# Attention and expert kernel: transpositions of softmax rows in halves, values pair by pair, one copy moved in ScalarE's list

## The chip, the cores and the metric

The kernel runs on one core of a Trainium2 chip. Its time is the device time of one execution in microseconds; given is the median of three runs. TensorE multiplies matrices and writes to PSUM, VectorE, ScalarE and GpSimd (POOL in the profile) work on SBUF and PSUM, and SyncE issues transfers. Each engine runs its own list in order; semaphores join the lists.

## What is computed

```python
xn = _layernorm(x, axis=-1)                      # x: 8 batches x 256 rows x 128
q, k, v = ...                                    # 16 heads of 64; k, v from a latent of 64
q = q * cos + _rotate_half(q) * sin              # the same for k
scores = q @ k.T / 8, causal mask
probs = softmax(scores)
s = (probs @ v).reshape(...) @ wo.T
g = silu(TOP_K * expert_of_each_row(xn))         # one of 8 experts, 128 -> 512 -> 128
out = x + s * g
```

All of it is float32. The change touches the step from `probs` to `probs @ v`.

## The kernel before

Work goes by **pairs** of heads: 8 batches x 8 pairs = 64 pairs, numbered g = 0 to 63. Every engine has a hand-written list, made of one `slot(g)` per pair; what stands in a slot of one engine belongs to different pairs, so that the engines overlap. For one pair, with both heads i = 0, 1 and 256 rows in two blocks of 128 (the causal half leaves 128 + 256 = 384 columns, `SW`):

- `scores` (TensorE, L1187 and L1189): head i lies on partitions 64 i to 64 i + 63, so each multiplication uses 64 rows of the array, and the two heads stand side by side on its two halves. Results go to banks `s_bank[i]`.
- `row_max` (VectorE, L633) masks and takes the negated maximum of rows; `exponentials` (ScalarE, L975) makes `pexp` and the row sums, two instructions a head, each with the read-out of its sum; `denominators` (VectorE, L640) is the reciprocal; `scale` (GpSimd L499, ScalarE L988, or VectorE L651) writes `probs`. In the stage of the change ScalarE scales one quarter of a pair (128x128), GpSimd three.
- `turn` (TensorE, L1199) transposes `probs` in three blocks 128x128 a head into `t_bank[i]`; `turned_probs` (ScalarE, L997) copies each head's bank to `probsT`, one of four buffers.
- `values` (TensorE, L1216 and L1218) multiplies by the latents, two pairs at once, the two heads on the two halves of the array's columns; `ctx_out` (ScalarE, L1004) copies the result, `output` (TensorE, L1233) multiplies by the joined value and output weights.
- `project` (TensorE, L1161 to L1178) makes rotary inputs of a pair eight later, VectorE (L617, L624) and GpSimd (L488) rotate, SyncE stores (L388).

Pairs 0 to 39 come first, then the experts, then pairs 40 to 63. **Periods** (`PERIODS` = 42, 44, ..., 56) join the slots of an even pair s and of s + 1 into one list on TensorE (`period`, L1335): scores s + 2; values of s - 2 and s - 1; scores s + 3; `turn(s)`; projection s + 8; outputs s - 2 and s - 1; `turn(s + 1)`; projection s + 9. In period 42 `turn(42)` stands before scores 45 and no values are computed. Projections end with 63.

ScalarE's slot g (L1085): exponentials of g + 1 for head 0; exponentials of g + 1 for head 1; in an even slot of a period the context copy of g - 2; `turned_probs(g)`; its quarter of `scale(g + 1)`. GpSimd's slot: its parts of `scale(g + 1)`, in even slots a rotation, and from slot 43 to 58 one gather of gate rows (L515). VectorE's slot in a period: `row_max(g + 2)`, rotation, `denominators(g + 1)`; in a few slots two instructions of a finished batch.

Of the kernel before, what the change touches and what calls it, by code (L numbers as in the profile page):

```python
# [16 lines left out]
P = 128  # L17
# [42 lines left out]

LATE = B * NP - 2
VECTOR_CTX = (LATE - 6, LATE - 4)


def values_through(g):
# [50 lines left out]
def build(nc, x, wqT, w_dgT, w_kupT, w_vup, woT, gate_b, w1, b1, w2, b2,  # L116
          c_rot, c_ident, c_mask, c_before, c_expert, c_excl, c_incl, c_tile, out):
    with ExitStack() as ctx:
# [207 lines left out]
        def take_turns(eng, g, i, k):  # L326

            if g and scaler(g - 1, i, k) != scaler(g, i, k):
                eng.wait_ge(probs_ready[i][k], g)

        def turned_to(u):

# [635 lines left out]
        def _(act):  # L968
# [22 lines left out]
            def turned_probs(g):  # L991

                if g > 3:
                    act.wait_ge(pv_done, values_through(g - 4))
                for i in range(2):
                    act.wait_ge(probsT_done, 2 * g + i + 1)
                    act.copy(probsT[:, g % 4, i, :], t_bank[i][:, 0:SW]).then_inc(probsT_ready, 1)  # L997
# [87 lines left out]
            def slot(g):  # L1085
                if g in (4, 8, 12):
                    turned(g // 4 + 1)
                if g in (5, 9, 13):
                    latents_high(g // 4 + 1)
                if g in (7, 11, 15):  # L1090
                    latents_copied(g // 4)
                if g == COUNT_SLOT + 1:
                    act.wait_ge(cnt_done, 1)
                    act.copy(counts[:], w_bank[:, 0:(NT + 1) * E]).then_inc(cnt_read, 1)
                more = g + 1 < B * NP and g != G_LEAD
                if g == G_LEAD:
                    act.wait_ge(e_done, NR)
                    turned_probs(g)
                    exponentials(g + 2, 0)
                    turned_probs(g + 1)  # L1100
                    exponentials(g + 2, 1)
                    half_tanh(NR - 1, 1)
                more = more and g != G_LEAD + 1
                if more:
                    exponentials(g + 1, 0)
                if g > 1 and g - 2 in ALONE and g not in (G_LEAD, G_LEAD + 1):
                    ctx_out(g - 2)
                if g % 2 and g > 2 and g - 3 not in ALONE and g < LATE - 3 and g != G_LEAD + 1 and not in_period(g):
                    ctx_out(g - 3)
                if more:  # L1110
                    exponentials(g + 1, 1)
                if g in PERIODS:
                    ctx_out(g - 2)
                if g == LATE:
                    ctx_out(g - 2)
                if g == LATE + 1:
                    act.wait_ge(probsT_ready, 2 * g)
                if g not in (G_LEAD, G_LEAD + 1, LATE):
                    turned_probs(g)
                if g + 1 < B * NP and g != G_LEAD:  # L1120
                    scale(g + 1)
                if g in (2, 6, 10):
                    normalise(g // 4 + 2)
                if g in (5, 9, 13):
                    logits_out(g // 4 + 1)
# [31 lines left out]
        def _(pe):  # L1157
# [33 lines left out]

            def turn(g):

                for i in range(2):
                    wait(pe, probsT_ready, 2 * g + i - 1)
                    for k in range(3):
                        if k < 2:
                            pe.wait_ge(probs_ready[i][k], g + 1)
                        t = pe.transpose(t_bank[i][:, k * P:(k + 1) * P], probs[:, g % 2, i, k * P:(k + 1) * P], ident[:])  # L1199
                    t.then_inc(probsT_done, 1)  # L1200

            def values(g):
# [6 lines left out]
                    pe.wait_ge(rope_done, B * NP)  # L1209
                else:  # L1210
                    wait(pe, ctx_ready, values_through(min(g, LATE)) - 1)
                pe.wait_ge(probsT_ready, 2 * (g + n))
                pairs = slice(g % 4, g % 4 + n)
                o = (w_bank if g == LATE else o_bank)[:, 0:n * S].rearrange("p (n s) -> p n s", s=S)
                for i, r in enumerate(half_rows):
                    pe.matmul(o[r, :, :], lat_all[:, 2 * b, :], probsT[:, pairs, i, 0:S], start=True, stop=False)  # L1216
                for i, r in enumerate(half_rows):
                    m = pe.matmul(o[r, :, P:S], lat_all[:, 2 * b + 1, :], probsT[:, pairs, i, S:SW], start=False, stop=True)  # L1218
                m.then_inc(pv_done, 1)

            def output(g):
# [113 lines left out]
            def period(s):  # L1335
# [11 lines left out]
                    output(s - 3)  # L1347
                output(s - 2)
                output(s - 1)
                turn(s + 1)  # L1350
                for m in items(s + 1):
                    project(m)
                for m in items(s)[1:]:
                    project(m)

            def slot(g):
                if in_period(g):
# [21 lines left out]
                if g == G_LEAD:  # L1379
                    turn(g + 1)  # L1380
                elif g == G_LEAD + 1:
                    values(g - 1)
                else:
                    turn(g)
                if g in (3, 7, 11):
                    turn_rows(g // 4 + 2)
# [11 lines left out]
                    values(g - 1)  # L1398
                if g > 1 and g % 2 == 0 and g - 2 not in ALONE and g not in (G_LEAD, G_LEAD + 2):
                    values(g - 2)  # L1400
                for m in items(g)[1:]:
                    project(m)

# [85 lines left out]
```

## Time and profile before

| | |
|---|---|
| median of 3 runs | 302.62 us (302.54 to 303.06) |
| the profiled execution's own time | 303.29 us |
| its span in the trace | 301.5 us |
| TensorE busy / instructions | 289.6 us (96%) / 2362 |
| ScalarE busy | 239.3 us (79%) |
| VectorE busy | 229.7 us (76%) |
| GpSimd busy | 213.5 us (71%) |
| TensorE's granted clock | 1.00 in all stretches |

The page gives busy times over the whole span, the costliest groups of instructions, and what ended the idle time before them. A table by stage gives the same for chosen stretches. The view in order of time lists instructions with start and duration in us, neighbours of one kind merged ("x6"); a group's time runs from its first start to its last end. Multiplications overlap in these records, so a group of n has n - 1 steps and one record's length. The stage of the change lies from about 226 us to 278 us.

### The profile page before, as it was taken

To read this page: it belongs to the slowest core of one execution; us is meant where nothing else is said; L and a number is where in the kernel's file an instruction comes from. 1 tells how busy PE (TensorE), PEld (TensorE's weight loads), DVE (VectorE), ACT (ScalarE), POOL (GpSimd) and SP (SyncE) were. 2 spreads that over 40 slices of the span, in tenths; PEclk is the share of its full clock that TensorE was granted. 3 is DMA by queue.
4 is the path that set the end of the run, shared out by engine and by line. 5 is a ranking of instruction groups with operands and counts; after the bars stand their busy time and mean duration, and the time that the engine had idled before them with its cause. 6 is when DMAs were issued, how large, how long until landed. Compare 5 with 4: busy or idle time off the path is not lost.

```text
span 301.5 us, 8603 instructions
## 1 busy us (share of the span) xinstructions
PE 289.6 (96%) x2362; PEld 235.0 (78%) x2362; DVE 229.7 (76%) x909; ACT 239.3 (79%) x863; POOL 213.5 (71%) x325
## 2 busy tenths in 40 slices
PE   8798999999999999999999989999999999999994
PEld 2576888888888888777776779999977778887663
DVE  4889998987777898988898723444377889898981
ACT  4278789898887889989998676677787898999971
POOL 2478878697778669999999982333226899998730
PEclk9999999999999999999999999999999999999999
DMA  6864685879333233444333382000234243543410
GB/s 192 249 133 115 114 276 148 205 194 300 87 75 68 60 75 83 107 101 102 90 97 90 112 245 55 2 0 2 66 93 108 64 113 99 121 106 109 113 37 17
DMA packets 39596, 33.35 MB, mean 111 GB/s; under 512 B 4801, under 2 KB 36674, under 8 KB 39554
## 3 DMA queue, kind: packets, MB, share of 16 engines
q1 hardware_dynamic: 38098, 30.51, 39.8%
q0 software_dynamic: 1024, 2.10, 2.4%
q8 instruction: 20, 0.33, 0.5%
q10 hardware_dynamic: 432, 0.23, 0.3%
q14 instruction: 22, 0.18, 0.2%
HBM read 11.07 MB, written 4.98 MB: 53 GB/s over the span
## 4 chain that ended last, share of the span: by engine, by line
PE 64%; POOL 14%; DVE 9%; issue 6%; DMA 3%; ACT 1%; POOLq 0%; SPq 0%; DVEq 0%; ACTq 0%
PE bank L1199 9%; PE bank L1187 9%; PE bank L1216 8%; PE bank L1450 7%; PE bank L1438 6%; PE bank L1233 6%; POOL probs L499 5%; POOL staged L488 5%; PE bank L1161 3%; DVE rot_out L617 3%; PE bank L1218 3%; PE bank L1189 3%; POOL xn L515 3%; DMA qk_sb<-staged 3%; DVE masked L633 2%
## 5 line engine op out<-in xcount | busy, mean ns | idle before, releaser
L975 ACT ACTIVATE pexp<-masked,negmax 128x128 f32<-128x128 f32 (+1 forms) x256 | 113.9, 452 | 2.2 <-DVE negmax L633 2.2
L499 POOL TENSOR_SCALAR probs<-pexp,rden 128x128 f32<-128x128 f32 (+1 forms) x195 | 84.3, 447 | 27.0 <-DVE rden L640 25.2
L633 DVE CUSTOM_DVE_ANT_0 masked<-bank,mask 128x128 f32<-128x128 f32 (+1 forms) x256 | 75.9, 352 | 21.4 <-PE bank L1189 20.5
L488 POOL TENSOR_TENSOR staged<-rot_out 128x512 f32<-128x512 f32 x56 | 71.4, 1278 | 16.2 <-DVE rot_out L617 15.6
L617 DVE TENSOR_TENSOR rot_out<-bank,rot 128x1024 f32<-128x1024 f32 x64 | 77.7, 1215 | 4.6 <-PE bank L1163 3.5
L997 ACT COPY probsT<-bank 128x384 f32<-128x384 f32 x126 | 54.0, 480 | 27.3 <-PE bank L1199 26.0
L1199 PE MATMUL bank<-ident,probs 128*128 128x128 f32 x384 | 54.0, 275 | 0.7 <-issue 0.5
L975 ACT ACTIVATION_READ_ACCUMULATOR pexp<-masked,negmax 128x1 f32 x256 | 50.0, 195 | 0.0
L1187 PE MATMUL bank<-qk_sb 64*128 64x256 f32 x256 | 47.0, 428 | 1.7 <-DMA qk_sb<-staged 1.3
L1199 PEld LDWEIGHTS bank<-ident,probs 128*128 128x128 f32 x384 | 43.0, 140 | 3.4 <-issue 1.2
L1233 PE MATMUL bank<-vo_sb,ctxT 128*128 128x128 f32 x256 | 37.8, 278 | 0.7 <-ACT ctxT L1004 0.7
L1216 PE MATMUL bank<-probsT,lat_all 128*64 128x256 f32 (+1 forms) x184 | 37.7, 487 | 0.0
L1145 ACT ACTIVATE probsT<-bank,w_own 128x128 f32<-128x128 f32 x88 | 25.0, 369 | 12.9 <-PE bank L1438 12.9
L1233 PEld LDWEIGHTS bank<-vo_sb,ctxT 128*128 128x128 f32 x256 | 33.0, 191 | 1.8 <-ACT ctxT L1004 1.1
L1187 PEld LDWEIGHTS bank<-qk_sb 64*128 64x128 f32 x256 | 20.6, 184 | 16.4 <-issue 11.6
L575 POOL COPY w_own<-w_sb 128x516 f32 x22 | 14.9, 678 | 23.6 <-ACT probsT L1145 23.6
L1189 PEld LDWEIGHTS bank<-qk_sb 64*128 64x128 f32 x256 | 26.1, 187 | 2.8
L1189 PE MATMUL bank<-qk_sb 64*128 64x128 f32 x256 | 26.8, 272 | 0.0
L954 DVE TENSOR_TENSOR z<-bank,b_all 128x128 f32 (+1 forms) x22 | 6.4, 292 | 24.2 <-PE bank L1450 21.7
L1218 PEld LDWEIGHTS bank<-probsT,lat_all 128*64 128x64 f32 x184 | 13.6, 137 | 13.9 <-issue 9.9
L1450 PE MATMUL bank<-w_sb,probsT 128*128 x176 | 23.3, 276 | 0.3 <-ACT probsT L1145 0.3
L1438 PE MATMUL bank<-probsT,w_own 128*128 128x128 f32 x176 | 23.3, 276 | 0.0
(117 smaller groups left out, 483.6 us busy)
## 6 DMA issues: line engine op xcount, KB each, us to landing
qk_sb<-staged SPq DMA_DIRECT2D x128, 128.0 KB
w_sb<-in_w SPq DMA_DIRECT2D x2, 1024.0 KB, 5.8
w_sb<-in_w SPq DMA_DIRECT2D x4, 512.0 KB, 5.3
sorted_x<-z SPq DMA_DIRECT2D x1, 1408.0 KB, 8.0
sorted_g<-z SPq DMA_DIRECT2D x1, 1152.0 KB, 5.5
out<-res SPq DMA_DIRECT2D x8, 128.0 KB, 2.3
x_sb<-in_x SPq DMA_DIRECT2D x3, 256.0 KB, 3.8
rot<-in_c_rot SPq DMA_DIRECT2D x1, 512.0 KB, 5.7
```

What stands on the lines that cost most here:

```text
L488: pool.tensor_tensor(staged[:, n % 2, :, m % 2, :], rot_out[:, m % 2, :, 0:S], rot_out[:, m % 2, :, S:2 * S], op=ALU.add).then_inc(staged_ ...
L499: pool.tensor_scalar(probs[:, g % 2, i, c], pexp[:, g % 2, i, c], rden[:, g % 2, i, k:k + 1], 1.0, ALU.mult, ALU.mult).then_inc(probs_read ...
L617: dve.tensor_tensor(rot_out[:, m % 2], bank_of(m)[:].unsqueeze(1).broadcast_to([P, 2, 2 * S]), rot[:], op=ALU.mult).then_inc(rope_done, 1)
L633: t = dve.tensor_tensor_reduce(masked[:, g % 2, i, c], s_bank[i][:, c], mask[:, c], -1.0, -NEG * 1e8, ALU.add, ALU.min, negmax[:, g % 2, i ...
L975: e = act.activation(pexp[:, g % 2, i, c], masked[:, g % 2, i, c], ACT.Exp, bias=negmax[:, g % 2, i, k:k + 1], scale=-1.0, accum_out=rowsu ...
L997: act.copy(probsT[:, g % 4, i, :], t_bank[i][:, 0:SW]).then_inc(probsT_ready, 1)
L1187: pe.matmul(s_bank[i][:, P:SW], qk_sb[r, 0, p, P:S], qk_sb[r, 1, p, :], start=True, stop=True)
L1189: m = pe.matmul(s_bank[i][:, 0:P], qk_sb[r, 0, p, 0:P], qk_sb[r, 1, p, 0:P], start=True, stop=True)
L1199: t = pe.transpose(t_bank[i][:, k * P:(k + 1) * P], probs[:, g % 2, i, k * P:(k + 1) * P], ident[:])
L1216: pe.matmul(o[r, :, :], lat_all[:, 2 * b, :], probsT[:, pairs, i, 0:S], start=True, stop=False)
L1233: m = pe.matmul(y_bank[:, i * C:(i + 1) * C], ctxT[:, p, i * P:(i + 1) * P], vo_sb[:, p, :], start=(p == 0 and i == 0), stop=(p == NP - 1) ...
L1450: m = pe.matmul(bank[6 + i][:, 0:C], hidT[:, i, k, :], w2_sb[:, k, :, :].rearrange("p e c -> p (e c)")[:, bass.ds(e * C, C)], start=(k == ...
```

## The change

1. `HALVED` holds pairs 43 to 56. For these `turn` transposes 64 rows at a time, twelve instructions instead of six; rows 0 to 63 of both heads go to `t_bank[0]`, rows 64 to 127 to `t_bank[1]`. ScalarE's two copies each wait for all transpositions of the pair and write strips of 64 columns.
2. `TURN_LAST` holds 43, 45, ..., 55. In `period` their `turn` moves from before to behind the projections, so that it stands next to the scores of the next period.
3. `values` of a joined couple (42, 43), ..., (54, 55) is split: first the even pair, after its copies, then the odd pair, after its own.
4. In ScalarE's list `turned_probs` of an odd pair moves from its own slot to the next one, between the exponentials of head 0 and head 1.

```diff
+TURN_LAST = (*range(PERIODS[0] + 1, PERIODS[-1], 2),)
+HALVED = (*TURN_LAST, *PERIODS[1:])
...
+        def turned_half(g, i):
+
+            whole = probsT[:, g % 4].rearrange("p i (k q c) -> p (i k) q c", q=2, c=HD)
+            return whole[:, :, i, :]
...
+                if g in HALVED:
+                    act.wait_ge(probsT_done, 2 * g + 2)
+                    for i in range(2):
+                        act.copy(turned_half(g, i), t_bank[i][:, 0:SW].rearrange("p (n c) -> p n c", c=HD)
+                                 ).then_inc(probsT_ready, 1)
+                    return
...
+                if g - 1 in TURN_LAST:
+                    turned_probs(g - 1)
                 if more:
                     exponentials(g + 1, 1)
...
-                if g not in (G_LEAD, G_LEAD + 1, LATE):
+                if g not in (G_LEAD, G_LEAD + 1, LATE) and g not in TURN_LAST:
                     turned_probs(g)
...
+                if g in HALVED:
+                    wait(pe, probsT_ready, 2 * g)
+                    for i in range(2):
+                        for k in range(3):
+                            if k < 2:
+                                pe.wait_ge(probs_ready[i][k], g + 1)
+                            for o, r in zip(t_bank, half_rows):
+                                t = pe.transpose(o[:, (3 * i + k) * HD:(3 * i + k + 1) * HD],
+                                                 probs[r, g % 2, i, k * P:(k + 1) * P], ident[r, r])
+                        t.then_inc(probsT_done, 1)
+                    return
...
-                pe.wait_ge(probsT_ready, 2 * (g + n))
-                pairs = slice(g % 4, g % 4 + n)
...
+                parts = ((g, 1), (g + 1, 1)) if g in PERIODS and g + 1 in TURN_LAST else ((g, n),)
+                for j, k in parts:
+                    pe.wait_ge(probsT_ready, 2 * (j + k))
+                    pairs = slice(j % 4, j % 4 + k)
+                    at = slice((j - g) * S, (j - g + k) * S)
...
-                turn(s + 1)
+                if s + 1 not in TURN_LAST:
+                    turn(s + 1)
                 for m in items(s + 1):
                     project(m)
                 for m in items(s)[1:]:
                     project(m)
+                if s + 1 in TURN_LAST:
+                    turn(s + 1)
```

Two more conditions on `TURN_LAST` stand in the ordinary slot of TensorE.

## Rows read from the trace of the kernel before

**Rows 1.** The page, busy time by engine (share of the span) and instructions.
```profile
PE 289.6 (96%) x2362; PEld 235.0 (78%) x2362; DVE 229.7 (76%) x909; ACT 239.3 (79%) x863; POOL 213.5 (71%) x325
```
**Rows 2.** Table by stretch, one period: length, busy by engine (PE, PEld, DVE, ACT, POOL), clock.
```profile
245.35:252.07 6.72, 6.72 (x56) 5.35 (x55) 5.80 (x23) 6.17 (x25) 6.33 (x10) 1.00 0.40 99
```
**Rows 3.** TensorE in order of time, 243.2 to 249.2: start, length, instructions.
```profile
243.24 1.05 PE L1233 MATMUL bank<-vo_sb,ctxT 128*128 128x128 f32 x8
244.13 0.82 PE L1199 MATMUL bank<-ident,probs 128*128 128x128 f32 x6
...
245.88 0.39 PE L1189 MATMUL bank<-qk_sb 64*128 64x128 f32 x4
246.24 1.08 PE L1216 MATMUL bank<-probsT,lat_all 128*64 128x512 f32 x4
247.12 0.63 PE L1218 MATMUL bank<-probsT,lat_all 128*64 128x256 f32 x4
247.68 0.70 PE L1187 MATMUL bank<-qk_sb 64*128 64x256 f32 x4
248.21 0.39 PE L1189 MATMUL bank<-qk_sb 64*128 64x128 f32 x4
248.53 0.87 PE L1199 MATMUL bank<-ident,probs 128*128 128x128 f32 x6
249.16 0.36 PE L1161 MATMUL bank<-xnT_h,wq_h 128*128 128x256 f32 x1
```
**Rows 4.** ScalarE in order of time, 242.4 to 249.2.
```profile
242.45 0.86 ACT L997 COPY probsT<-bank 128x384 f32<-128x384 f32 x2 [0.56 <-PE bank L1199]
243.19 0.41 ACT L988 ACTIVATE probs<-pexp,rden 128x128 f32<-128x128 f32 x1
243.50 0.40 ACT L975 ACTIVATE pexp<-masked,negmax 128x128 f32<-128x128 f32 x1
...
245.16 0.19 ACT L975 ACTIVATION_READ_ACCUMULATOR pexp<-masked,negmax 128x1 f32 x1
245.25 0.83 ACT L997 COPY probsT<-bank 128x384 f32<-128x384 f32 x2
...
249.17 0.86 ACT L997 COPY probsT<-bank 128x384 f32<-128x384 f32 x2 [0.55 <-PE bank L1199]
```
**Rows 5.** All transpositions L1199: ns minimum/median/maximum, first and last start.
```profile
L1199 PE MATMUL bank<-ident,probs x384: 270/273/331, 23.6 to 294.3; 128*128 128x128 f32 x192
```
**Rows 6.** Weight loads of the 8-row transpositions L1268: one group of four; one load's ns.
```profile
18.41 0.32 PEld L1268 LDWEIGHTS bank<-ident,z 8*128 8x128 f32 x4
...
L1268 PEld LDWEIGHTS bank<-ident,z x16: 133/136/138, 18.4 to 80.7; 8*128 8x128 f32 x16
```
**Rows 7.** TensorE in order of time: a projection that follows scores directly.
```profile
221.41 0.38 PE L1161 MATMUL bank<-xnT_h,wq_h 128*128 128x256 f32 x1
221.63 0.28 PE L1162 MATMUL bank<-xnT_l,wq_h 128*128 128x256 f32 x1
221.75 0.28 PE L1163 MATMUL bank<-xnT_h,wq_l 128*128 128x256 f32 x1
```
**Rows 8.** Reciprocals on VectorE and a scaling of ScalarE that waited for one.
```profile
245.39 0.18 DVE L640 RECIPROCAL rden<-rowsum 128x4 f32<-128x4 f32 x1
...
232.09 0.17 DVE L640 RECIPROCAL rden<-rowsum 128x4 f32<-128x4 f32 x1
...
232.35 0.40 ACT L988 ACTIVATE probs<-pexp,rden 128x128 f32<-128x128 f32 x1 [0.19 <-issue]
```
**Rows 9.** Copies of pairs 44 and 56; transpositions of 58 and GpSimd's scaling before them.
```profile
235.72 0.86 ACT L997 COPY probsT<-bank 128x384 f32<-128x384 f32 x2 [0.76 <-PE bank L1199]
...
276.11 0.86 ACT L997 COPY probsT<-bank 128x384 f32<-128x384 f32 x2 [0.56 <-PE bank L1199]
...
279.40 1.61 PE L1199 MATMUL bank<-ident,probs 128*128 128x128 f32 x6
...
279.68 0.83 POOL L499 TENSOR_SCALAR probs<-pexp,rden 128x128 f32<-128x128 f32 x2
```

## What the change should do to the time

> **What bounds the kernel now.** I read the busy shares first, then a table by stage, then one period of TensorE and one of ScalarE line by line. By the page TensorE is busy for 289.6 of 301.5 us [rows 1], so any instruction taken from it looks like time won. The stage that the change touches is the eight "periods" (pairs 42 to 57, about 226 to 278 us). One of them takes 6.72 us: TensorE busy 6.72, GpSimd 6.33, ScalarE 6.17, VectorE 5.80 [rows 2]. So TensorE is full, but nothing behind it has more than 0.6 us to spare, and the question is what is late next.
>
> The list of TensorE [rows 3] and that of ScalarE [rows 4] answer it. I name the pairs of one period: scores 50 ending with the group at 245.88, values 46 and 47 at 246.24, scores 51 at 247.68, transpositions of 48 at 248.53, projection at 249.16. Outputs (243.24) and the transpositions of 47 (244.13) stand before. ScalarE copies the transposed pair 46 at 242.45, scales a quarter of 47, takes the four exponentials of 48, and copies 47 at 245.25. The second of these copies ends at 245.25 + 0.83 = 246.08, and the values start 0.15 us later. So a loop runs through both engines:
>
> copies of 46 begin 242.45; ScalarE without a gap to 246.08 (3.63); hand-over 0.15; values 46/47 1.44 (246.24 to 247.68); scores 51 0.85 (to 248.53); transpositions of 48 until ScalarE copies them 0.64 (to 249.17). Sum 6.71, which is the period. TensorE itself waits only about 0.04 us in it: from the last score to the values it takes 0.24 us (245.88 + 0.39 - 0.27 = 246.00 to 246.24), from the last score to the transpositions, where nothing is awaited, 0.20 (248.33 to 248.53). TensorE's own list (about 6.68) and this loop (6.72) are level. An edit that shortens TensorE's list wins only if it leaves the loop alone.
>
> **The change, part by part.**
>
> *Transpositions by row halves.* For the 14 pairs 43 to 56, six transpositions 128x128 become twelve of 64 rows, two at a time on the two halves of the array. Now one takes a step of 0.109 us: (0.82 - 0.27) / 5, where 0.27 is the recorded time of one multiplication (the group at 244.13) [rows 3, 5]. The operand that streams, the identity, halves from 128 to 64 columns: 0.055. The weights loaded stay 128 columns wide. The nearest row is the group of transpositions with 8 rows and 8 columns: its weight loads alone make a step of (0.32 - 0.14) / 3 = 0.06 us [rows 6]. I take 0.061 for a step of two halves, because scores, which are already such pairs, show two halves as one step (four 128-column multiplications of 64 rows in 0.39, that is one further step of 0.11 after the first) (at 248.21) [rows 3]. Six steps: 0.37 for 0.65, so -0.29 per pair. Bounds: 0.055 a step if the load hides; 0.12 a step if the halves go one after the other, which is +0.07 instead of -0.29.
>
> The Trainium skill, "TensorE: Matmul & The Clock Gate", Part 3, says that a weight load overlaps a running matmul only when its row group differs. By that rule load and stream of one half would add up, about 0.11 a step, and nothing would be won in a transposition: 0.3 us more in the loop below. In this trace a full-array transposition loads new weights in the same rows every time, which alone takes 0.06 [rows 6], and still goes at the 0.11 that 128 columns cost in the scores [rows 3]; so the load is hidden, and the trace speaks against the rule here.
>
> *Their places.* Changing between full array and halves costs an emptying plus an uncovered weight load. Last score to first transposition is 0.20 us (248.21 + 0.39 - 0.27 = 248.33 to 248.53) for a step of 0.11, so 0.09, and the first transposition then takes 0.05 more (0.87 for six against 0.82) [rows 3]. After the change the transpositions of an even pair follow scores without a switch, and the switch comes before the projection, whose first step is 0.22 (221.41 to 221.63) for 0.12 in the next one (to 221.75) [rows 7]: 0.10, where the transposition had paid 0.05, so 0.05 dearer. For an odd pair the switch moves from before the scores to before the transpositions, and what the loads cost there is a wash. The number of switches, four a period, is the same. TensorE's list: 6.68 - 2 x 0.29 + 0.05 = 6.15 us, and 0.01 for the split below: 6.16.
>
> *Values pair by pair.* Four multiplications of 512 and four of 256 columns become eight of 256 and eight of 128; the columns are the same. In one piece they take 1.44 (0.88 from 246.24 to 247.12 and 0.56 to 247.68). The second pair alone is half of the streamed part plus the switch to the scores: steps of 0.24 and 0.22 for 256 columns, 0.11 for 128, and 0.24 from the last one to the scores, 0.80 in all (half of 1.44, and 0.08 for the switch that does not halve). The first pair needs only copies made long ago, the second those of the odd pair.
>
> *ScalarE's copies.* Copies of an odd pair leave the end of its own slot and go between the two heads of the next slot's exponentials. The list becomes: copies 46, quarter scale 47, exponentials 48, quarter scale 48, first head's exponentials of 49, copies 47, second head's, context copy, copies 48. Two things now stand ahead of copies 47 that stood behind. First, quarter scale 48 follows the exponentials of 48 directly, while its reciprocal on VectorE needs the last row sum. That ends at 245.16 + 0.19 = 245.35, 0.10 after ScalarE's next instruction could start (245.25) [rows 4]; the reciprocal can follow 0.03 later, as now at 245.39, and takes 0.18 [rows 8]; from its end to ScalarE's scaling is 0.08 where ScalarE stood waiting for just this (232.09 + 0.17 to 232.35) [rows 8]. So 0.39 us of ScalarE standing still, which copies 47 used to fill; bounds 0.3 and 0.5 (VectorE must have its rotation and sum before the reciprocal done by then; today they end just as the row sum does, and the projection that they wait for comes no later). Second, the scaling 0.31 (243.19 to 243.50) and half of 1.75 for the exponentials, 0.88 (243.50 to 245.25) [rows 4].
>
> Both copies of a halved pair wait for all of its transpositions, since each bank now holds half the rows of both heads. The start is no later, though: 5 x 0.061 + 0.22 (the 0.27 less the 0.055 of half the columns) + 0.10 for the hand-over (today the third transposition ends 248.53 + 0.05 + 0.22 + 0.27 = 249.07, the copy starts 249.17) = 0.63 after the first transposition, for 0.64 now. The copies write six strips of 64 instead of 384 in a row; no row shows that form, I take it at the price of a plain copy, with 0.1 us a pair as the upper bound and no gain below.
>
> *The new loop*, all from [rows 3, 4, 8]. Copies 46 0.74; scale 0.31; exponentials 48 1.75; standing still 0.39; scale 0.31; exponentials 49, first head 0.88; copies 47 0.83: 5.21 on ScalarE. Hand-over 0.15. Then on TensorE second pair of the values 0.80; scores 51 0.75 (0.85 less the switch after it, 0.10); transpositions of 48 to the copy 0.63. Sum **7.54 us** for 6.72 now. Taken out: the first pair of the values (0.64) and a switch. Put in: 0.39 + 0.31 + 0.88 = 1.58. TensorE, with 6.16 of work, would stand about 1.4 us a period before the values of the odd pair, and behind that wait are queued the scores, the next transpositions and projections, so nothing of it is made up.
>
> *How often, and the ends.* From the copies of 44 (235.72) to those of 56 (276.11) [rows 9] are six periods, 6.73 each: 6 x 0.81 = +4.9. In the first one (42 to 44) the quarter scale of 44 starts at 232.35 as now [rows 8], then 0.31 + 0.88 + 0.83 + 0.15 + 0.80 + 0.75 + 0.63 puts the copies of 44 at 236.70 instead of 235.72: +1.0. After the last one, now, the six transpositions of pair 58 take 1.61 us instead of 0.87, waiting for GpSimd's scaling, which stands behind a gather and ends at 279.68 + 0.83 [rows 9]. In longer periods GpSimd is no longer behind, and that wait goes in part; but the exponentials of 58 stay tied to the copies of 56, so I give back 0.4 (0 to 0.7). The other edits (conditions in the ordinary slots) touch no pair: 43 to 55 all lie in periods.
>
> Sum: 4.9 + 1.0 - 0.4 = +5.5. The profiled execution took 303.29 us (span 301.5 and 1.8 around it), which is 0.7 above the median 302.62 of the runs. On the median: **308.1 us**.
>
> **The rivals.**
> *Faster: TensorE's list is all that counts.* Mechanism: the split of the values covers the later copies, and each period shrinks to TensorE's 6.16. Then 7 x -0.56 and the 0.4 of the end: 298.3 us. For it: TensorE shows no idle time in the stage [rows 2]. Against it: it decides on whether copies 47 are done before the first pair of the values ends. Those end about 4.0 us after copies 46 began, and the copies at 5.21; 1.2 us of ScalarE's list would have to be absent.
> *Between: ScalarE's own list is the limit*, 6.17 of work plus 0.39 of standing still, 6.56 a period, if the two engines could drift apart: 7 x -0.16 - 0.4, 301.1 us. Against it: copies 48 cannot start before transpositions 48, which stand behind the values in TensorE's order.
> *Slower still: the halves go one after the other.* The even pair's transpositions lie in the loop: 6 x (0.12 - 0.06) = +0.36 in each of seven periods, 310.6 us; with the strips dearer as well, 311.3.
> That the change does not do what it says I find nowhere: the pairs named are those that the period's list issues.
>
> **How the numbers follow.** Forecast (period 7.4 to 7.7): 0.80, its own range 306.8 to 309.3. Halves in turn or dear copies: 0.10, near 310.6. TensorE's list alone: 0.05. ScalarE's list, or something near no change: 0.05. The range for 8 in 10 is 306.2 to 310.8. A measurement of this kernel can tell some 0.2% (0.6 us) from no change: faster 0.08, same 0.03, slower 0.89.
>
> **What would show it.** In the changed profile: starts of the copies of an even pair 7.5 us apart; TensorE idle 1.2 to 1.5 us inside the values, between a multiplication of 128 columns and one of 256, released by ScalarE's copy; ScalarE still for 0.4 us before a quarter scale in odd slots and for some 0.7 before the copies of an even pair; transpositions in six steps of 0.06; no switch pause between scores and transpositions; TensorE's busy share well below 96% in this stage. It is wrong if the odd pair's copies end before the first values do, if the reciprocal comes early enough to leave no pause, or if a step of two halves is not near 0.06.

## The result and the profile after

| | before | changed |
|---|---|---|
| median of the runs, us | 302.84 (302.54 to 303.38, 4 runs) | **307.54** (307.19 to 307.96, 4 runs) |
| ratio, 95% interval | | 1.0152 (1.0136 to 1.0168) |
| span of the profiled execution, us | 301.5 | 306.1 |
| TensorE busy, us | 289.6 | 287.9 |
| one period, us | 6.73 | 7.40 |
| from the copies of pair 44 to those of 56, us | 40.39 | 44.43 |

The changed kernel is 1.5% slower. The median of the kernel before is 302.84 here, for 302.62 ahead of the prediction, because a fourth run is counted. TensorE has 1.7 us less to do, and the span is 4.6 us longer.

On the page of the changed kernel the lines that answer to [rows 1] are these. The second is the group of the 256-column value multiplications, with the idle time of TensorE ahead of them and what ended it.
```profile
PE 287.9 (94%) x2502; PEld 234.8 (77%) x2502; DVE 230.3 (75%) x909; ACT 240.5 (79%) x863; POOL 212.6 (69%) x325
...
L1247 PE MATMUL bank<-probsT,lat_all 128*64 128x256 f32 (+1 forms) x212 | 39.3, 449 | 7.1 <-ACT probsT L1007 7.1
```
The kernel before had no such line. Seven stops, one a period, are all released by ScalarE's copies of a halved pair (L1007). A table by stretch of one period (beside [rows 2]) and of one stop inside it (length, busy by engine, clock):
```profile
244.01:251.41 7.41, 6.39 (x75) 5.27 (x76) 6.50 (x24) 6.39 (x23) 5.90 (x9) 1.00 0.32 90
247.94:249.23 1.28, 0.27 (x6) 0.03 (x3) 1.28 (x7) 1.28 (x6) 1.13 (x3) 1.00 0.79 257
```
No engine is busy for more than 6.5 of the 7.4 us. The period is a loop, not a full engine. TensorE in order of time in that period, to be laid beside [rows 3] (L1218 are the halved transpositions, L1204 and L1206 the scores, L1247 and L1249 the values, L1178 and L1179 a projection):
```profile
246.12 0.58 PE L1218 MATMUL bank<-ident,probs 64*128 64x64 f32 x12
246.54 0.65 PE L1204 MATMUL bank<-qk_sb 64*128 64x256 f32 x4
247.03 0.38 PE L1206 MATMUL bank<-qk_sb 64*128 64x128 f32 x4
247.34 0.65 PE L1247 MATMUL bank<-probsT,lat_all 128*64 128x256 f32 x4
247.83 0.39 PE L1249 MATMUL bank<-probsT,lat_all 128*64 128x128 f32 x4
249.23 0.65 PE L1247 MATMUL bank<-probsT,lat_all 128*64 128x256 f32 x4 [1.01 <-ACT probsT L1007]
249.71 0.39 PE L1249 MATMUL bank<-probsT,lat_all 128*64 128x128 f32 x4
250.03 0.70 PE L1204 MATMUL bank<-qk_sb 64*128 64x256 f32 x4
250.56 0.39 PE L1206 MATMUL bank<-qk_sb 64*128 64x128 f32 x4
250.79 0.53 PE L1218 MATMUL bank<-ident,probs 64*128 64x64 f32 x12
251.25 0.39 PE L1178 MATMUL bank<-xnT_h,wq_h 128*128 128x256 f32 x1
251.47 0.28 PE L1179 MATMUL bank<-xnT_l,wq_h 128*128 128x256 f32 x1
```
Six steps of halves take (0.53 - 0.22) / 5 = 0.06 each. Between the first pair's values and the second's lies the stop: their first step would have come at 247.83 + 0.22 = 248.05, and comes at 249.23, so **1.18 us a period** are lost. ScalarE, beside [rows 4], shows where it was meanwhile, and VectorE's reciprocal, beside [rows 8], what ScalarE stood for:
```profile
244.01 0.86 ACT L1007 COPY probsT<-bank 128x384 f32<-128x384 f32 x2 [0.68 <-PE bank L1218]
244.76 0.41 ACT L997 ACTIVATE probs<-pexp,rden 128x128 f32<-128x128 f32 x1
245.06 0.40 ACT L984 ACTIVATE pexp<-masked,negmax 128x128 f32<-128x128 f32 x1
...
247.16 0.40 ACT L997 ACTIVATE probs<-pexp,rden 128x128 f32<-128x128 f32 x1 [0.24 <-DVE rden L649]
247.47 0.39 ACT L984 ACTIVATE pexp<-masked,negmax 128x128 f32<-128x128 f32 x1
...
248.34 0.83 ACT L1007 COPY probsT<-bank 128x384 f32<-128x384 f32 x2
...
251.41 0.48 ACT L1007 COPY probsT<-bank 128x384 f32<-128x384 f32 x1 [0.68 <-PE bank L1218]
...
246.95 0.18 DVE L649 RECIPROCAL rden<-rowsum 128x4 f32<-128x4 f32 x1
```
The ends of the stage, beside [rows 9]: the copies of 44 and of 56, the transpositions of 58 and GpSimd's scaling before them.
```profile
236.60 0.48 ACT L1007 COPY probsT<-bank 128x384 f32<-128x384 f32 x1 [0.68 <-PE bank L1218]
...
281.03 0.48 ACT L1007 COPY probsT<-bank 128x384 f32<-128x384 f32 x1 [0.68 <-PE bank L1218]
...
284.32 1.07 PE L1227 MATMUL bank<-ident,probs 128*128 128x128 f32 x6 [0.71 <-ACT probsT L1012]
...
283.95 0.95 POOL L508 TENSOR_SCALAR probs<-pexp,rden 128x128 f32<-128x128 f32 x2
```
So the 4.6 us of the span are: 0.88 up to the copies of 44 (236.60 for 235.72), 4.04 in six periods (44.43 for 40.39), and -0.32 behind the copies of 56 (306.1 - 281.03 = 25.07 for 301.5 - 276.11 = 25.39).

### The profile page after: what moved, and what is told of

It reads as the page before. It is cut to its first block, busy times and chain, and to the rows that moved or that the text cites. A ratio compares the mean times of both kernels' runs of the same rounds, so it can differ in the third digit from the quotient of the medians.

```text
span 306.1 us, 8869 instructions
## 1 busy us (share of the span) xinstructions
PE 287.9 (94%) x2502; PEld 234.8 (77%) x2502; DVE 230.3 (75%) x909; ACT 240.5 (79%) x863; POOL 212.6 (69%) x325
## 4 chain that ended last, share of the span: by engine, by line
PE 65%; ACT 9%; DVE 9%; issue 8%; POOL 6%; DMA 1%; POOLq 0%; SPq 0%; ACTq 0%; DVEq 0%
PE bank L1204 9%; PE bank L1227 8%; PE bank L1247 8%; PE bank L1487 7%; PE bank L1475 6%; ACT pexp L984 6%; PE bank L1265 6%; PE bank L1178 3%; PE bank L1206 3%; DVE rot_out L626 3%; PE bank L1249 3%; DVE masked L642 3%; POOL staged L497 3%; POOL probs L508 2%; PE bank L1333 2%
## 5 line engine op out<-in xcount | busy, mean ns | idle before, releaser
L1012 ACT COPY probsT<-bank 128x384 f32<-128x384 f32 x98 | 42.1, 481 | 21.6 <-PE bank L1227 20.9
L1204 PE MATMUL bank<-qk_sb 64*128 64x256 f32 x256 | 46.5, 425 | 1.0 <-DMA qk_sb<-staged 0.5
L1247 PE MATMUL bank<-probsT,lat_all 128*64 128x256 f32 (+1 forms) x212 | 39.3, 449 | 7.1 <-ACT probsT L1007 7.1
L1227 PE MATMUL bank<-ident,probs 128*128 128x128 f32 x300 | 42.1, 275 | 1.2 <-ACT probsT L1012 0.7
L1227 PEld LDWEIGHTS bank<-ident,probs 128*128 128x128 f32 x300 | 33.6, 140 | 3.2 <-ACT probsT L1012 0.9
L1204 PEld LDWEIGHTS bank<-qk_sb 64*128 64x128 f32 x256 | 20.6, 185 | 13.1 <-issue 10.2
L1206 PEld LDWEIGHTS bank<-qk_sb 64*128 64x128 f32 x256 | 26.0, 187 | 2.9
L1206 PE MATMUL bank<-qk_sb 64*128 64x128 f32 x256 | 26.6, 271 | 0.0
L1249 PEld LDWEIGHTS bank<-probsT,lat_all 128*64 128x64 f32 x212 | 15.3, 137 | 12.3 <-issue 6.3
```

Source lines behind the costliest of these rows:

```text
L1204: pe.matmul(s_bank[i][:, P:SW], qk_sb[r, 0, p, P:S], qk_sb[r, 1, p, :], start=True, stop=True)
L1206: m = pe.matmul(s_bank[i][:, 0:P], qk_sb[r, 0, p, 0:P], qk_sb[r, 1, p, 0:P], start=True, stop=True)
```

## The experiments

"Period" below is a sixth of the time from the copies of pair 44 to those of 56 in the trace of the kernel named. A stop is idle time of TensorE ahead of values. Ratios are to the kernel before, run on the same chip.

### Which part does what

**The move of the copies, alone**, put into the kernel before:
```diff
+                if g - 1 in TURN_LAST:
+                    turned_probs(g - 1)
                 if more:
                     exponentials(g + 1, 1)
...
-                if g not in (G_LEAD, G_LEAD + 1, LATE):
+                if g not in (G_LEAD, G_LEAD + 1, LATE) and g not in TURN_LAST:
                     turned_probs(g)
```
`TURN_LAST` is defined as in the change and used nowhere else.

> The kernel before with the one edit that ScalarE copies an odd pair between the two heads of the next slot's exponentials; transpositions whole, in their old places, values of both pairs at once. Theory of the loop: 6.73 + 0.35 (ScalarE waits for the reciprocal) + 0.31 + 0.88 = 8.25 us a period, +1.5 in each of seven: 313 us (312 to 314). Rival (TensorE's order and splitting cost the time, ScalarE's place does not matter): within 1 us of 302.8.

Measured: 313.1 us, ratio 1.0349 (1.0322 to 1.0376). The period is 8.24 us, the stops 1.5 to 1.7 us each (10.6 us in seven). The move alone costs 10 us; the halves, the split and the later place of the odd pair's transpositions together take half of that back.

**The changed kernel with whole transpositions** (`HALVED = ()`).

> The changed kernel with whole 128-row transpositions, their places, the split and ScalarE's order kept. Theory of the loop: only the even pair's transpositions lie in it, and there the first copy again needs the first head alone; 0.10 for the switch before them and about 0.01 in the hand-over, so the period is 7.5 us and the whole 308.3 us (307.8 to 308.8): the 0.28 us that the halves save per pair is nearly worthless here. Rival (the halves are what makes the changed kernel slow): below 305 us.

Measured: 308.24 us, ratio 1.018 (1.0158 to 1.0202), period 7.51 against 7.40. In the changed kernel the halves save 0.11 us in a period, though each pair's transpositions are 0.29 us shorter. Only the even pair's transpositions lie on the loop, and there a halved pair's copies wait for all its steps: scores with the switch behind them and transpositions until copied were 0.85 + 0.64 and are 0.75 + 0.63, which is this 0.11.

**The changed kernel with the values of both pairs in one piece**:
```diff
-                parts = ((g, 1), (g + 1, 1)) if g in PERIODS and g + 1 in TURN_LAST else ((g, n),)
+                parts = ((g, n),)
```


> The changed kernel with the values of both pairs computed at once again, when both copies are there. Theory of the loop: the first pair's 0.64 us comes back into the loop, and 0.1 for the switch after the scores: 7.40 + 0.7 = 8.1 us a period, 312.5 us. Rival (splitting costs something of its own): at or below 307.5 us.

Measured: 324.34 us, ratio 1.068 (1.062 to 1.074). 12 us more than expected. The table by stretch shows two stops with the values behind them (the column after GpSimd's is the granted clock):
```profile
231.70:233.90 2.20, 0.28 (x6) 0.11 (x3) 1.86 (x9) 2.15 (x8) 1.99 (x4) 1.00 0.27 55
233.90:236.70 2.80, 2.79 (x29) 1.79 (x30) 1.03 (x5) 1.34 (x5) 2.11 (x5) 1.00 0.08 23
...
239.80:242.00 2.20, 0.34 (x6) 0.15 (x2) 1.86 (x10) 2.12 (x8) 1.89 (x4) 0.97 0.63 202
242.00:244.90 2.90, 2.86 (x10) 0.96 (x10) 0.70 (x2) 0.79 (x4) 2.23 (x5) 0.50 0.12 29
```
and TensorE in order of time the price:
```profile
233.91 1.08 PE L1247 MATMUL bank<-probsT,lat_all 128*64 128x512 f32 x4 [1.93 <-ACT probsT L1007]
234.79 0.63 PE L1249 MATMUL bank<-probsT,lat_all 128*64 128x256 f32 x4
...
242.04 1.97 PE L1247 MATMUL bank<-probsT,lat_all 128*64 128x512 f32 x4 [1.90 <-ACT probsT L1007]
243.77 1.09 PE L1249 MATMUL bank<-probsT,lat_all 128*64 128x256 f32 x4
```
After the second stop the granted clock is 0.50, the lower level (1.2 of 2.4 GHz), and the same four multiplications take 243.77 - 242.04 = 1.73 us for 234.79 - 233.91 = 0.88. The two stops above are of the same length, and only the second lowered the clock, so the length alone doesn't say when. Of the seven stops (1.93, 1.90, 2.82, 2.21, 2.94, 2.98 and 1.95 us) the five in the middle are followed by values at the lower clock, the first and the last are not. Periods are 10.13 us on average (copies of 44 at 236.74, of 56 at 297.52), 2.73 more than in the changed kernel. Slower values make the loop longer. They don't by themselves make the next stop longer, since they put off its start as well as its end; why three of the later stops are near 3 us is not shown. Ahead of the 2.82 us, ScalarE's copies of 46 began 1.0 us behind the recorded end of their transpositions (246.31 to 247.33), where 0.10 is usual.

To see if the clock explains the whole excess, the same kernel with **seven dummy multiplications** in the stop:
```diff
                 parts = ((g, n),)
+                if g in PERIODS and g + 1 in TURN_LAST:
+                    keep_warm(7, o_bank)
```


> Edit: the changed kernel with the values of each couple of pairs in one piece again (as in the variant without the split), and seven dummy multiplications of 512 columns on TensorE ahead of them, where it would stand still for 2.2 to 2.9 us; their sums are overwritten. Theory: of the 17 us that the kernel without the split lost against the changed one, some 5 us are ScalarE's longer loop (values of 1.44 us instead of 0.80 behind the copies), and the rest is the granted clock of 0.50 behind the long stops, so that keeping TensorE busy gives about 312.5 us at a clock of 1.00. Rival, that the loop itself is that long and the clock fell for lack of work: 322 to 325 us.

Measured: 311.91 us, ratio 1.0299 (1.0283 to 1.0315). Added work made it 12.4 us faster. The same stretches:
```profile
239.80:242.00 2.20, 2.00 (x15) 0.80 (x11) 1.86 (x10) 2.11 (x8) 1.89 (x4) 1.00 0.69 209
242.00:244.90 2.90, 2.90 (x30) 1.83 (x31) 1.24 (x5) 1.50 (x6) 2.24 (x5) 1.00 0.11 30
```
The period is 8.04 us, 0.64 more than the changed kernel's, and 0.64 is just what the loop gains with joined values (1.44 behind the copies for 0.80). Seven periods of it are 4.5 us, for 4.4 between 311.9 and 307.5.

### What in ScalarE's list makes the loop long

**The quarter scaling behind the copies of the odd pair**, where the changed kernel has it ahead of the exponentials of head 0:
```diff
                 if g - 1 in TURN_LAST:
                     turned_probs(g - 1)
+                    scale(g)
...
-                if g + 1 < B * NP and g != G_LEAD:
+                if g + 1 < B * NP and g != G_LEAD and g not in TURN_LAST:
```


> Edit: the changed kernel, but in the odd slots ScalarE's quarter of the query scaling for the next slot goes behind the copies of the odd pair instead of ahead of the head 0 exponentials. My theory: in the changed kernel ScalarE's loop copies 46, scaling, exponentials 48, standing still, scaling, exponentials 49 head 0, copies 47, second values, scores 51, transpositions holds 7.40 us a period; this takes its standing still of 0.35 us and one scaling of 0.31 us out of it, so that the loop would be 6.75 us long, and the kernel 7.5 periods x 0.65 us = about 4.5 us shorter than the changed one: 303 us, or up to 304.5 us if VectorE or GpSimd holds the periods near the 6.85 us of the variant with the copies in their own slot. Rival, that TensorE's own longer list holds the period and ScalarE's list does not: 307.5 us, as the changed kernel.

Measured: 303.45 us, ratio 1.0015 (1.0003 to 1.0027), period 6.81. One scaling moved in ScalarE's list gives 4.1 of the 4.7 us back. The loop is still closed by ScalarE's copies, with stops of 0.4 us in place of 1.0 by the same kind of view (2.5 us in six for 7.1 in seven), as the list of what TensorE's matmuls waited for says (line, what for, us in total, times, longest):
```profile
PE bank L1248 <- ACT probsT L1007: 2.5, 6, 0.5
```
That confirms the standing still and the scaling as terms of the sum: 7.40 - 0.35 - 0.31 = 6.74, measured 6.81.

**The copies of the odd pair back in their own slot**, with the halves and the split values kept:
```diff
-                if g - 1 in TURN_LAST:
-                    turned_probs(g - 1)
...
-                if g not in (G_LEAD, G_LEAD + 1, LATE) and g not in TURN_LAST:
+                if g not in (G_LEAD, G_LEAD + 1, LATE):
```


> The changed kernel with ScalarE's copies of the odd pair back in their own slot, all else kept. Theory of the loop (ScalarE's list order costs the time): the copies end about 3.7 us after those of the even pair began and the first values about 4.0 us after, so TensorE never waits in the values; the period falls from 7.40 to TensorE's own 6.23 us, or to 6.3 to 6.4 where GpSimd (6.33 busy before, with gaps of 0.16 around its gathers) is then the last: 298.5 to 300.5 us in all, clearly faster than before. Rival (the halves or the split values cost the time): no more than the stop of 1.2 us a period is shared out, and the time stays above 303 us.

Measured: 302.69 us, ratio 0.9991 (0.998 to 1.0002). The stop is gone: TensorE goes from the first pair's values to the second's without a wait. But with a list of 6.2 us it takes 6.85 a period, and the gain that the halves should bring doesn't come. A miss of 2 to 4 us, which the other runs were spent on.

### Where the gain of the halves goes

These start from the variant with the copies in their own slot, except the second.

**Without GpSimd's gathers** in the slots 43 to 58:
```diff
-                if GATHER_SLOT <= g < GATHER_SLOT + NT:
-                    gather(GATHER_ORDER[g - GATHER_SLOT])
...
-                dve.wait_ge(g_in[b], 32)
```


> Edit: the variant with the copies in their own slot, without GpSimd's gathers of the slots 43 to 58 (the expert outputs' row sums are then left out, so that the output is not the reference's) and without VectorE's wait for them. It asks what holds that variant's period at 6.85 us where TensorE's own list takes 6.2. If GpSimd (6.2 to 6.5 us busy in a period, some 2.4 us of it issuing gathers) is the limit, the period falls to 6.2 to 6.3 us and the time to about 299 us. If VectorE (5.5 to 7.1 us busy in a period) is, it stays at 6.8 us and the time at 302 to 303 us.

Measured: 300.11 us, ratio 0.9915 (0.9898 to 0.9932), period 6.34. Two of its periods:
```profile
234.78:240.96 6.18, 6.18 (x75) 5.29 (x76) 5.77 (x22) 6.17 (x23) 3.81 (x8) 1.00 0.30 64
240.96:247.13 6.17, 6.17 (x75) 5.29 (x76) 5.77 (x20) 6.17 (x23) 3.81 (x8) 1.00 0.49 104
```
TensorE is busy for all of them: 6.17 is its own list, which the prediction put at 6.16. In the whole table four of the six periods are 6.16 to 6.23; the other two, in which VectorE finishes batches, 6.6 and 6.7.

**The same cut in the kernel before.**

> Edit: the kernel before, without GpSimd's gathers of the slots 43 to 58 (the expert outputs' row sums are left out, so that the output is not the reference's) and without VectorE's wait for them. If the kernel before is held by TensorE's own list of 6.71 us a period, as the prediction says, GpSimd is off its path and the time stays at 302.5 to 303 us; the halves and the split values are then worth the difference to the 300.1 us of the same cut in the variant with the copies in their own slot. If GpSimd holds the kernel before too, it falls to about 300 us.

Measured: 302.62 us, ratio 0.9994 (0.9985 to 1.0003), period 6.73. The gathers cost the kernel before nothing. They cost the variant 2.6 us (302.69 - 300.11; 2.3 by the two ratios, since the runs were on different chips), so they use up nearly all that the halves, the split and the places of the transpositions would save (302.62 - 300.11 = 2.5 us, 2.4 by the ratios).

What is it about the gathers? Three shifts of work were tried.

**Finished batches later**: `FINALS = {50: 5, 57: 0, 58: 1, 59: 6, 60: 2, 61: 4, 62: 3}` for `{48: 0, 50: 5, 53: 1, 54: 2, 56: 3, 59: 6, 61: 4}`.

> Edit: the variant with the copies in their own slot, and VectorE's last steps of the finished batches 0 to 4 (0.95 us in each of the slots 48, 53, 54, 56, 61) put into the slots 57, 58, 60, 61 and 62, five of seven thus behind the periods' middle. If VectorE's share in the slots 48 to 56 holds that variant's period at 6.85 us, four steps of 0.95 us leave these slots and up to 3.8 us come back, less what the end then has more of: 299.5 to 301.5 us. If it is GpSimd or TensorE, 302.5 us as that variant; if the end is short of VectorE, 304 us.

Measured: 303.95 us, ratio 1.0031 (1.0011 to 1.005). The periods get hardly shorter (6.78 for 6.85), and what follows the copies of 56 gets 1.1 us longer (302.3 - 275.99 = 26.3 for 300.7 - 275.52 = 25.2). VectorE's last steps are not what the variant loses to.

**One scaling of GpSimd's to VectorE** in every even slot:
```diff
-            return "pool" if k or not busy else ("pool" if in_period(g - 1) else "vector", "scalar")[i]
+            return "pool" if k or not busy else ("pool" if in_period(g - 1) and g % 2 else "vector", "scalar")[i]
```


> Edit: the variant with the copies in their own slot, and in every even slot of the periods GpSimd's scaling of head 0's first 128 rows (0.38 us) given to VectorE, which stands still for about a microsecond behind that slot's reciprocals. Theory: GpSimd's list of six scalings, one rotation sum and two gathers with what is between them, 6.8 us, holds that variant's period; it gets 0.38 us shorter, so that 0.3 to 0.4 us in each of seven periods come back: 299.9 to 300.8 us. Rival, that GpSimd's finish of one scaling, not the length of its list, held TensorE, or that VectorE is late instead: 302 to 303.5 us.

Measured: 303.21 us, ratio 1.0014 (1.0004 to 1.0025), period 6.76. VectorE's scaling, beside a gather of GpSimd:
```profile
245.88 0.76 DVE L660 TENSOR_SCALAR probs<-pexp,rden 128x128 f32<-128x128 f32 x1
...
245.31 1.31 POOL L524 DMA_INDIRECT xn<-sorted_g,pos  x1 [0.16 <-issue]
```
It took 0.76 us, until the gather ended (245.31 + 1.31 = 246.62); the next one, which began at 252.79, 0.1 us ahead of a gather's end, took 0.29. A gather beside it doesn't always hold it: the scaling that began at 239.10, in the middle of a gather (238.48 to 239.80), took 0.29 as well. GpSimd's shorter list brought 0.1 us a period. GpSimd now waited 3.2 us for TensorE in this stage, so its list was not the limit; but VectorE, with the scaling added, was busy for 38.9 of the 40.6 us, so the run doesn't weigh GpSimd's list alone.

**The gathers spread** over the slots 43 to 62, with the finished batches 3, 6 and 4 a slot later.

> Edit: the variant with the copies in their own slot, and GpSimd's sixteen gathers spread over the slots 43 to 62 in place of 43 to 58, eleven in place of fifteen of them in slots of the periods; the finished batches 3, 6 and 4 one slot later each. If GpSimd's list holds that variant's period, four gathers of some 1.3 us with what lies around them leave the periods; no more than 0.65 us can come back in a period before TensorE's own list of 6.2 us binds, and the tail may give some of it back: 300.5 to 302 us. If the list isn't the limit: 302.7 us.

Measured: 305.43 us, ratio 1.0084 (1.006 to 1.0107). The period is 6.78, so fewer gathers in it help by 0.07; what follows the copies of 56 takes 29.5 us for 25.2. The chain that ended last leads there through a late gather's transfer (2.16 us from 282.61) to VectorE's step that reads it.

None of the three brought the 2.6 us back, but they don't clear GpSimd's list. Over the variant's six periods the table by stretch adds up to
```profile
sum 41.12, PE 39.71 PEld 33.26 DVE 37.38 ACT 37.11 POOL 37.64; mean PE 6.62 PEld 5.54 DVE 6.23 ACT 6.18 POOL 6.27
```
and GpSimd pauses for 0.16 us ahead of each of its twelve gathers, 1.9 us in all. That makes 39.5 us, or 6.59 a period, where TensorE's list needs 6.17: with two gathers a period GpSimd alone keeps the variant from 6.2. Of these 39.5 us, 1.1 are that four gathers took 1.31 or 1.32 us and not 1.03; each of the four began while VectorE's rotation sum was running. Without that GpSimd's list would take 6.40. The rest of the way, from 6.59 to 6.85, needs another cause, and the trace of the variant shows one. GpSimd, VectorE and the end of TensorE's scores of an even pair:
```profile
243.69 1.31 POOL L524 DMA_INDIRECT xn<-sorted_g,pos  x1 [0.16 <-issue]
...
244.16 0.18 DVE L649 RECIPROCAL rden<-rowsum 128x4 f32<-128x4 f32 x1
245.30 0.29 DVE L642 CUSTOM_DVE_ANT_0 masked<-bank,mask 128x128 f32<-128x128 f32 x1 [0.96 <-PE bank L1204]
...
244.14 0.39 PE L1204 MATMUL bank<-qk_sb 64*128 64x128 f32 x4
```
The scores are complete at 244.53, VectorE is free from 244.34, and its row maxima (which read the mask from SBUF and the scores from PSUM) begin at 245.30: 0.78 us late, 0.30 behind the gather's end. In the same kernel it happens at 238.49 (0.67 late), not at 258.58, where the gather began 0.74 us ahead of the scores' end, for 0.88 and 0.84 in the two held cases. In the changed kernel the gather of such a slot ends before the scores do, and the row maxima follow them by 0.05. In the kernel before the gather of this place is long too (1.50 us from 244.81), but it ends at 246.31, as the scores do (246.27), and the row maxima begin at 246.32: nothing is lost there, which fits that taking the gathers out of that kernel changed nothing. The view puts this wait down to the scores; the one other thing that the row maxima await, ScalarE's exponentials of two pairs before, had ended at 244.13. That the gather held them is read from the times, and no run shows it by itself.

**The gather ahead of GpSimd's rotation sum** was to take it out of that place:
```diff
+                if GATHER_SLOT <= g < GATHER_SLOT + NT:
+                    gather(GATHER_ORDER[g - GATHER_SLOT])
                 for m in rotations(g):
                     if m not in VECTOR_SUMS:
                         rotated(m)
```


> Edit: the variant with the copies in their own slot, and in the slots in which GpSimd has both, its gather goes ahead of its rotation sum of 1.27 us instead of behind it. In that variant's trace a gather lies across the end of an even pair's scores (gather 243.69 to 245.00, scores done 244.53), and VectorE, idle since 244.34, begins the row maxima 0.30 us behind the gather's end, 0.78 us behind the scores; without the gathers, and in the changed kernel, where the gather ends before the scores, the row maxima begin 0.05 us behind them. Theory: this hold, not the length of GpSimd's list, is what the gathers cost. With the gather ahead it lies at 242.3 to 243.4 and ends before the scores: the row maxima are held no more, up to 0.6 us in each of the periods where it happened (two to four of seven) come back, and the time is 300.2 to 301.7 us. Rival, the length of GpSimd's list or VectorE's as such: 302.3 to 303.5 us.

Measured: 306.07 us, ratio 1.011 (1.0093 to 1.0128), period 7.36. Both theories missed. GpSimd and VectorE:
```profile
243.83 1.03 POOL L524 DMA_INDIRECT xn<-sorted_g,pos  x1 [0.16 <-issue]
244.88 1.29 POOL L497 TENSOR_TENSOR staged<-rot_out 128x512 f32<-128x512 f32 x1
...
244.47 2.26 DVE L633 TENSOR_TENSOR staged<-rot_out 128x512 f32<-128x512 f32 x1
246.65 0.16 DVE L649 RECIPROCAL rden<-rowsum 128x4 f32<-128x4 f32 x1
246.74 0.25 DVE L642 CUSTOM_DVE_ANT_0 masked<-bank,mask 128x128 f32<-128x128 f32 x1
```
VectorE's own rotation sum, two operands in SBUF, takes 2.26 us here. In the kernel before its eight are:
```profile
L624 DVE TENSOR_TENSOR staged<-rot_out x8: 691/692/748, 11.8 to 272.1; 128x512 f32<-128x512 f32 x8
```
It began while the gather ran, GpSimd's sum followed the gather at once, and it ended 246.73 - 246.17 = 0.56 us behind the end of GpSimd's sum: most of its 0.69 us was done only then. The row maxima stand behind it, 1.06 us behind the scores. So the two engines don't work side by side in these pairings. This fits the Trainium skill, "SBUF — State Buffer", section "SBUF: two separate sides", which says of the shared port pair that VectorE or GpSimd holds it exclusively for a whole instruction and the other one blocks, and that VectorE needs it in a 2-port mode or, against a GpSimd operation that reads SBUF, with two inputs in SBUF. The two sums are such a case. The row maxima have one input in SBUF, and no view shows whether a 2-port mode was at work in them, so what held them stays open.

What stands after this: that the gathers cost the variant 2.6 us and the kernel before nothing is shown by taking them away. Three kinds of pairing in which VectorE was late or slow, by 0.5 to 1.6 us, are in the traces. How the 2.6 us split between GpSimd's own list (6.59 of 6.85 us a period) and such holds is not shown, since every run that moved or lightened something also loaded another place. No variant that computes everything beat the kernel before.

## Why the prediction was right, point by point

The forecast was 308.1 us in a range of 306.2 to 310.8; the changed kernel takes 307.54. The loop that it named is the one in the trace, and each of its terms can be read there:

| term of the loop | forecast | measured, from the rows of after |
|---|---|---|
| copies 46 | 0.74 | 244.01 to 244.76: 0.75 |
| quarter scaling 47 | 0.31 | 0.30 |
| exponentials 48, ScalarE's standing still | 1.75 + 0.39 | 245.06 to 247.16: 2.10 |
| quarter scaling 48 | 0.31 | 0.31 |
| exponentials 49, first head | 0.88 | 247.47 to 248.34: 0.87 |
| copies 47 | 0.83 | 0.83 |
| hand-over to the values | 0.15 | 249.17 to 249.23: 0.06 |
| values of 47 | 0.80 | 249.23 to 250.03: 0.80 |
| scores 51 | 0.75 | 250.03 to 250.79: 0.76 |
| transpositions of 48 until copied | 0.63 | 250.79 to 251.41: 0.62 |
| sum | 7.54 | 7.40 |

*Right*: the halved step at 0.061 (0.062); a halved pair copied no later and no dearer than a whole one; the switch gone between scores and transpositions (250.56 + 0.39 - 0.27 = 250.68 to 250.79, 0.11 for 0.20) and paid at the projection (251.25 to 251.47, 0.22 for 0.12); TensorE's own list at 6.16 (6.17 where nothing holds it); the first scaling of the odd slot exposed, because its reciprocal now has no copies to cover it; no sign of TensorE catching up behind the stop.

*Mis-sized terms.* The hand-over from ScalarE's copies to the values: 0.15 was taken from a place where TensorE had just finished other work. Now it already stands on the array form of the values, with the first pair's done, and it starts 0.06 behind the copy; that this is the reason is likely and not tested. Standing still: 0.35 for 0.39. Together 0.13, with rounding 0.14 a period, and 0.86 in six (4.04 for 4.9). The first loop gave 0.88 for 1.0, the tail -0.32 for -0.4. Sum 4.6 for 5.5; against the runs of the same chip 4.7.

*The rivals.* TensorE's list alone (298.3) and ScalarE's list as the limit (301.1) both needed the second copies to be off the loop: the stop of 1.18 us at each of them says that they are not. Halves in turn (310.6) fell with the step of 0.06. On the halved step the prediction weighed the Trainium skill, "TensorE: Matmul & The Clock Gate", Part 3, by which a weight load overlaps only a multiplication of another row group. Alone, a load of 128 columns takes 0.06 [rows 6] and the streamed half 0.055; added up the step would be near 0.11. It is 0.062, so here, too, the trace goes against that rule.

*What the prediction did not see* is what would have happened without the move. It took for granted that TensorE's 6.16 us list would set the pace if only the loop did not (298.3 for the rival). With the copies in their own slot the time is 302.69, not near 298.3. The busy times of a period [rows 2] had GpSimd at 6.33 and ScalarE at 6.17, already as long as the list hoped for. With the pauses ahead of its gathers, two of 0.16 a period, GpSimd's list takes 6.6, and the pairings of its gathers with VectorE come on top. Even without the gathers the time was 300.11, in part because two of the six periods stayed at 6.6 and 6.7. This did not touch the forecast, since the longer loop left room for both.

## What to carry to other kernels

When a wait is split so that the first half can start early, ask what now stands ahead of the second half's producer: here a pause, one more scaling and half of the exponentials came ahead of the copies, and moving that one scaling behind them was worth 4.1 us. Before shortening the busiest engine, add up the others over the same stretch, with the pauses between their instructions: a list cut from 6.7 to 6.2 us brings little when a neighbour needs 6.6. If a stop of about two microseconds in TensorE can't be avoided, look at the granted clock behind it; dummy work in seven such stops was worth 12.4 us here.

## What the runs showed of the hardware

- The granted clock stayed at 1.00 over stops of 1.2 us (changed kernel) and 1.5 to 1.7 us (the move alone), and fell to 0.50 behind five of the seven stops of 1.90 to 2.98 us with joined values, though not behind the two of 1.93 and 1.95 us. Four value multiplications of 512 columns then took 1.73 us for 0.88. Seven dummy multiplications in each stop kept the clock at 1.00 and brought 12.4 us back.
- A gather that GpSimd issues took 1.03 to 1.08 us, and 1.31 to 1.50 us where VectorE's rotation sum, with two operands in SBUF, was running as it began: four times each in the stage of the variant and of the kernel before.
- VectorE's scaling of 128x128 took 0.76 us beside a gather for 0.29, but 0.29 beside another one; VectorE's sum of two SBUF operands took 2.26 us beside GpSimd's gather and sum for 0.69. VectorE's reciprocal of four columns took its usual 0.18 us inside a gather.
- Two transpositions of 64 rows on the two halves of the array take 0.062 us together, for 0.109 of a whole one, with the weights of the same rows loaded anew each time.
